# Products on still operands in three idle places of TensorE, in a Perceiver layer with a mixture of experts

## The reference

```python
x = x + relu(softmax_attention(norm(x), ctx, W, b) @ W.T + b)      # cross attention
x = x + attn(norm(x))    # causal linear attention, 16 heads of 64, then gelu FFN 512-2048-512
x = x + moe(norm(x))     # 8 experts, top 2

router_logits = x @ w_router
top_w, top_i = jax.lax.top_k(router_logits, K)
top_w = softmax(top_w)
gating = zeros((t, e)).at[arange(t)[:, None], top_i].add(top_w)
for ei in range(e):
    hmid = silu(x @ w0[ei]) * (x @ w1[ei])
    out = out + gating[:, ei:ei + 1] * (hmid @ wo[ei])
```

## Time and profile before

| | us |
|---|---|
| median of 3 runs | 699.74 |
| lowest, highest of them | 698.71, 931.4 |
| the profiled execution, whole | 702.32 |
| its span, first to last instruction | 700.6 |

### The profile page before, as it was taken

The page is one execution under the profiler, slowest core; times in us unless marked ns, Lnnn a source line. Parts: engine busy times, 40 slices in busy tenths (PEclk is TensorE's granted clock), DMA queues, the critical chain, the costliest instruction groups (busy, mean ns, idle before and its releaser), DMA issues.

```text
span 700.6 us, 9558 instructions
## 1 busy us (share of the span) xinstructions
PE 651.6 (93%) x3370; PEld 538.0 (77%) x3371; DVE 426.5 (61%) x688; ACT 372.8 (53%) x523; POOL 252.9 (36%) x172
## 2 busy tenths in 40 slices
PE   4979998998998999989969999969999999999994
PEld 4868886886876788878758888768888888888883
DVE  8566666656677545576776354845475463762775
ACT  4499986986973254430142244322574555754850
POOL 5078885776894424340000022123022020220233
PEclk9999998998999999999989999969999999999998
DMA  8435453343041612221080793316599191991925
GB/s 324 187 120 175 148 182 129 121 138 118 9 143 60 198 61 90 83 98 62 1 279 22 242 403 120 120 46 238 182 353 373 53 360 46 356 371 66 341 84 176
DMA packets 51844, 116.95 MB, mean 167 GB/s; under 512 B 5208, under 2 KB 5208, under 8 KB 48736
## 3 DMA queue, kind: packets, MB, share of 16 engines
q1 hardware_dynamic: 47360, 106.51, 43.2%
q10 hardware_dynamic: 3168, 5.77, 2.4%
q0 software_dynamic: 1280, 4.20, 1.8%
HBM read 102.31 MB, written 14.16 MB: 166 GB/s over the span
## 4 chain that ended last, share of the span: by engine, by line
PE 78%; DVE 12%; ACT 3%; issue 3%; DMA 2%; POOL 1%; SPq 0%; POOLq 0%; DVEq 0%; ACTq 0%
PE bank L1351 18%; PE bank L1353 18%; PE bank L1352 18%; PE bank L1365 5%; PE bank L1416 3%; PE bank L1417 3%; PE bank L1384 3%; PE bank L1385 3%; PE bank L1750 1%; PE bank L1580 1%; PE bank L1401 1%; PE bank L1730 1%; PE bank L1568 1%; DVE xn L984 1%; PE bank L1737 1%
## 5 line engine op out<-in xcount | busy, mean ns | idle before, releaser
L466 POOL TENSOR_TENSOR nat_lo<-raw,nat_hi 128x512 fp32r<-128x512 f32 x104 | 134.3, 1315 | 55.9 <-ACT nat_hi L584 55.3
L515 POOL TENSOR_TENSOR e_lo<-e_raw,e_hi 128x2048 fp32r<-128x2048 f32 x9 | 41.6, 4619 | 230.2 <-ACT e_hi L743 230.2
L863 DVE TENSOR_TENSOR ct_lo<-bank,ct_hi 128x512 fp32r<-128x512 f32 x96 | 65.9, 689 | 48.7 <-ACT ct_hi L551 48.4
L1351 PE MATMUL bank<-w_hi,turned 128*128 128x512 f32 x176 | 70.7, 402 | 4.0 <-DVE turned L990 2.6
L551 ACT ACTIVATE ct_hi<-bank 128x512 fp32r<-128x512 f32 x96 | 57.1, 596 | 26.4 <-PE bank L1365 24.5
L1352 PE MATMUL bank<-w_lo,turned 128*128 128x512 f32 x176 | 69.5, 395 | 0.0
L1353 PE MATMUL bank<-w_hi,turned 128*128 128x512 f32 x176 | 69.4, 394 | 0.0
L584 ACT ACTIVATE nat_hi<-raw 128x512 fp32r<-128x512 f32 x104 | 65.0, 629 | 0.0
L1365 PE MATMUL bank<-ident,raw 128*128 128x128 f32 x384 | 61.1, 285 | 0.0
L1351 PE MATMUL bank<-e_hi,turned 128*128 128x512 f32 x144 | 59.0, 409 | 1.5 <-issue 1.5
L1365 PEld LDWEIGHTS bank<-ident,raw 128*128 128x128 f32 x384 | 50.1, 147 | 12.7 <-issue 1.2
(11 more groups left out here) (252 smaller groups left out, 1449.8 us busy)
## 6 DMA issues: line engine op xcount, KB each, us to landing
raw<-in_ctx_dram SPq DMA_DIRECT2D x24, 1024.0 KB, 5.0
w_raw<-in_L_ffn_w_dram SPq DMA_DIRECT2D x24, 1024.0 KB, 5.4
e_raw<-in_L_ffn_wo_dram SPq DMA_DIRECT2D x16, 1024.0 KB, 7.4
w_raw<-in_L_attn_w_dram SPq DMA_DIRECT2D x8, 1024.0 KB, 5.2
e_raw<-in_L_ffn_w_dram SPq DMA_DIRECT2D x8, 1024.0 KB, 7.4
slots_x<-zeros SPq DMA_DIRECT2D x1, 4096.0 KB, 16.9
slots_y<-zeros SPq DMA_DIRECT2D x1, 3840.0 KB, 26.2
vectors<-slots_x ACTq DMA_DIRECT2D x11, 256.0 KB, 5.0
```

The source lines that it names most:

```text
L466: nc.gpsimd.tensor_tensor(nat_lo[:, j, :], raw[b % 2][:, j, :], nat_hi[:, j, :].bitcast(f32), ALU.subtract).then_inc(nat_lo_ready, 1)
L515: nc.gpsimd.tensor_tensor(e_lo[j][:, :, :], e_raw[j][:, :, :], e_hi[j][:, :, :].bitcast(f32), ALU.subtract).then_inc(e_lo_ready[j], 1)
L863: nc.vector.tensor_tensor(ct_lo[:, n % CR, :], src, ct_hi[:, n % CR, :].bitcast(f32), ALU.subtract).then_inc(t_lo, 1)
L1351: nc.tensor.matmul(dst, lh, rh, start=first and k == 0, stop=False)
```

## The change

A helper is added to TensorE's block that issues the same product a number of times, with no semaphore raised. It is called at three places. 16 times ident x ident into bank 0, behind the wait for `const_ready` and ahead of the first wait for `pn`. 11 times a 128 x 128 part of `e_hi[4]` with a 512-wide row of it into bank 6, behind the last router product and ahead of the wait for DVE's choice; ahead of them stands a wait for the split of that unit. 5 times the same, behind the rank products and ahead of the wait for `in_first`. Bank 0 is written next by `context_turned`, bank 6 by `down_half`, both with start=True, so that nothing reads the results.

```diff
+            def keep_busy(count, dst, left, right):
+
+                for _ in range(count):
+                    nc.tensor.matmul(dst, left, right, start=True, stop=True)
+
             pe.wait_ge(const_ready, 1)
+            keep_busy(16, TB[0][:, 0:P], ident[:, :], ident[:, :])
             for t in range(NT):
                 pe.wait_ge(pn_ready, t + 1)
...
             routed(2)
             routed(3).then_inc(logits_done, 1)
+            pe.wait_ge(e_hi_ready[4], turn_of(0, 4))
+            keep_busy(11, bank[6][:, :], e_hi[4][:, 0, 0:P], e_hi[4][:, 1, :])
             pe.wait_ge(chosen_ready, 1)
             pe.wait_ge(order_ready, 2)
...
             mm.then_inc(rank_done, 1)
 
+            keep_busy(5, bank[6][:, :], e_hi[4][:, 0, 0:P], e_hi[4][:, 1, :])
             pe.wait_ge(chosen_ready, 2)
```

## The result

The changed kernel takes 703.3 us (median; 702.89 to 704.87), the kernel before 698.98 us beside it: a ratio of 1.0068, with a 95% interval of 1.0051 to 1.0085, or 3.6 to 5.9 us slower. The forecast was 699.2 us in a range of 695.8 to 702.9. The kernel is slower, where it was to be a little faster, and its time lies outside the range; that it would stay within 2% of the kernel before did come true.

What follows compares the result with a forecast made beforehand. TensorE's work and clock were taken as the bound, with half clock at the start and in the routing. Start +1.6 and routing -2.1 gave -0.5 us: 701.8 us, or 699.2 on the median's scale, range 695.8 to 702.9.

Steps and rivals of the forecast that it cites:

- The sixteen at the start: Start: 32 records, 6.8 us, under DVE's work; transposes at full clock, then 2.8 us idle ahead of an unmoved first product.
- I take +1.6: Start: the longer idle time lets the clock fall for 3.4 us across the first products, +1.6 us, bounds 0 to +2.7.
- the row with the nearest gap: Start: 2.66 us of standing still at 211.30 was followed by 3.41 us at half clock, taken as model for the 2.8 us gap.
- DVE ends this wait: Start: the first weight product waits for DVE until 15.45 us, so faster transposes gain nothing on the chain.
- The eleven: First routing wait: half clock, 4.7 us, 1.9 us too long for the 2.74 us wait; full clock from 463.1 us.
- the sum of the routing: Routing: late ranks, then ranks and gather at full clock; gather ends at 469.4 us instead of 471.56, -2.1 us.
- The step that failed: First routing wait: only the rank product queues behind the eleven on TensorE, and DVE waits for that; nothing further was priced.
- a slowing of DVE by TensorE: Second routing wait: excluded, as DVE's four lane tiles took 0.87 us beside an idle TensorE and 0.88 beside a busy one.
- Rival 1: Routing: clock stays half through the eleven, ranks and much of the gather, +1.6 us; with the start +3.2, 702.9 us; chance 0.30.
- Rivals 2 and 3: Routing clock never falls, 695.5 us, chance 0.15; start keeps full clock, late ranks cancel gather gain, 699.7 us, chance 0.15.
- The sign set for a wrong account: Whole kernel: a difference of more than 5 us would mean the clock in these places is not the whole story.
- The scale: Whole kernel: profiled execution 702.32 us, median 699.74, so 2.6 us was taken off the forecast of 701.8 us.

Runs made afterwards that it cites:

- e9: Changed kernel with five instead of eleven products in the first wait and DVE's split of unit 2 ahead of the logits wait; ratio to the kernel before 0.9985.
- e3: Changed kernel without the sixteen products at the start, so eleven and five in the routing only; 702.96 us, ratio to the kernel before 1.0067.
- e4: Changed kernel without the sixteen and the five, so the eleven products alone; 700.87 us, ratio to the kernel before 1.0032.
- e6: Changed kernel with DVE's split of unit 2 moved ahead of its wait for the router's logits; 698.74 us, ratio to the kernel before 0.9974.
- e8: Changed kernel with five products instead of eleven in the first wait; 699.27 us, ratio to the kernel before 0.9991.
- e10: Changed kernel with twenty-two products instead of eleven in the first wait; 705.59 us, ratio to the kernel before 1.0076.
- e11: Changed kernel with DVE's split of unit 2 ahead of the logits wait and unit 3 in the wait for ranks; ratio to the kernel before 0.9982.
- e12: Changed kernel with five instead of eleven products in the first wait and DVE's splits of units 2 and 3 both moved; ratio to the kernel before 0.9988.
- e1: The kernel before, profiled once more with no edit; 699.21 us, ratio 0.9999.
- e7: The kernel before with DVE's split of unit 2 moved ahead of its wait for the router's logits; ratio to the kernel before 1.0015.
- e2: Changed kernel with the sixteen products at the start alone, without the eleven and the five; ratio to the kernel before 0.9995.

## Why the prediction was wrong

**The sixteen at the start.** The duration (6.8 us foretold, 6.59 measured) and the unmoved first product are right. The idle time came out as 2.07 us instead of 2.8, since the context's transposes waited 1.48 us for their DMA, and the clock stayed full. The term "I take +1.6" was 0 in this profile. Going by the row with the nearest gap was no proof: idle times of 2.07 and 2.31 us left the clock alone, one of 2.01 us (e9) and one of 2.66 us (rows 8) were followed by half clock. e9 shows the term at its full 1.6 us, so its size was right, but it is there in some executions only. That DVE ends this wait holds for some only, too: in seven of the fourteen profiles (e3 and e4 without the sixteen, e6, e8, e10, e11 and e12 with them) DVE's two `W_lo` instructions took 1.3 us together instead of the 2.3 to 3.4 of the others, and the first product came between 13.45 and 14.72 us, right behind TensorE's transposes.

**The eleven.** Right: half clock when they begin, 4.6 us long, the ranks at 4.65 us behind the router instead of 2.74, full clock just as they end.

**The five, the ranks and the gather.** Right: the sum of the routing was -2.1 us and measured -1.7 (T to P).

**The step that failed** is in the part on the eleven: "What is queued behind them on TensorE is the rank product, and DVE waits for that." That is where the prediction stopped following the path, and the rest of it stood in the sum at nothing. DVE makes the slots of the ranks, GpSimd scatters by the slots, SP loads the second block behind the scatters, and TensorE needs that block 12 us behind P. From the end of the router products to the landing of the rows the kernel before takes 484.0 - 458.5 = 25.5 us, the changed one 485.1 - 456.8 = 28.3 us: 1.9 for the late ranks, -1.1 for their shorter products, 2.1 for the longer train of scatters. The last of these terms is against one profile of the kernel before; against e1 it is 1.0. The sum counted a gain up to P as a gain of the kernel, though the rows that TensorE needs 12 us behind P were 1.0 us early at most. What stood at nothing measured +5.7 us (P to Q): 3.9 of waiting, 1.6 of half clock behind it, and 0.2 that is not accounted for. I excluded a slowing of DVE by TensorE and never asked about GpSimd and DVE.

**Rival 1** gave 702.9 us and came nearest, but its mechanism is not what happened. It let the clock stay down through the ranks; the clock came back, and the loss lay 20 us further on. That its time is near is luck. **Rivals 2 and 3** did not occur, but for the full clock at the start that rival 3 had. The sign set for a wrong account, a difference of over 5 us, would not have shown it: the difference was 4.3 us, and the clock was still not the whole story. **The scale**: the 2.6 us between the profiled execution and the median were carried over as if they were fixed. They are one draw out of a spread of 7 us, so differences of single spans say little here.

## What to carry to other kernels

Filling an idle engine is free only as long as the filler fits the wait at the slow clock too, and a wait is only worth shortening if what it leads to is not held by another chain. Before counting a gain, follow each result of the stretch to its last user, its DMAs included, and note by how much that one was early: here 1.0 us at most. Where a train of indirect DMAs on GpSimd is waited for, long DVE instructions with two operands are best kept away from it; where it is not waited for, moving one gave nothing (e7).

## What the runs showed of the hardware

An indirect DMA issued by GpSimd (one of the scatters from the third on) took 0.96 us with no split beside it, 2.77 us when one DVE subtraction of 128 x 2048 ran across it (e6), and 4.97 us when it was held through two (changed kernel, e10). Each held one ended 0.83 to 0.86 us behind the end of such a subtraction, in some profiles while the next one was running.

The granted clock was half for 3.41 us behind an idle time of 3.89 us. Behind idle times of 2.0 to 2.3 us at the same place it fell in one profile (2.01 us, e9) and stayed full in others (2.07 us in the changed kernel, 2.31 us in e2). Ten runs of one unchanged program spread over 7 us in 700, and the profiles show half-clock stretches of 3.4 or 6.8 us at the same place of the program.

The records of `ident` times `ident` at the start of the changed kernel, with nothing else on TensorE, took 421 ns and more up to 6.9 us and 275 ns at the end: the clock rose while they ran.
